# Where the feed-forward products leave their banks: behind the slot's end or behind the next slot's first step

## What is computed

```python
x = x + ln(linear_attention(ln(x)))                    # 16 heads, decay, rope
x = x + ln(ffn_int(ln(x)))                             # silu(x Wg) * (x Wu), then Wd; width 2048
x = x + ln(causal_softmax_attention(ln(x)))            # 32 heads of 16, 8 key heads, rope
x = x + ln(gated_sequence_layer(ln(x)))                # row steps, gate
```

## Time and profile before

| | us |
|---|---|
| median of 3 runs | 4023.44 (4017.86 to 4025.12) |
| the profiled execution | 4021.19 |
| its span | 4019.4 |
| granted clock of TensorE, mean | 0.959 |
| PE busy | 3665.5 (91%) |
| DVE busy | 2540.6 (63%) |
| ACT busy | 1504.4 (37%) |
| POOL busy | 1458.0 (36%) |

### The profile page before, as it was taken

One profiled execution on the slowest core, in us unless ns is written; L12 is line 12 of the kernel. 1 busy time (PEld: TensorE's weight loads), 2 busy tenths in 40 slices (PEclk: granted clock), 3 DMA queues, 4 the chain that ended last, 5 costly groups with the idle time before them and its releaser, 6 DMA issues.

```text
span 4019.4 us, 51225 instructions
## 1 busy us (share of the span) xinstructions
PE 3665.5 (91%) x18536; PEld 2701.6 (67%) x18536; DVE 2540.6 (63%) x4046; ACT 1504.4 (37%) x2349; POOL 1458.0 (36%) x1802
## 2 busy tenths in 40 slices
PE   6878899999999999999999999999999999977678
PEld 5756776677767776677767776677767776654323
DVE  6754667566764767567664766566765766466347
ACT  4423433434242434434242434434243434315124
POOL 3421452245323552245323542255323542232114
PEclk9989999999999999999999999999999999987789
DMA  6456534254324533354324433353325432332304
GB/s 244 170 196 254 199 126 146 93 201 162 137 90 157 188 117 137 105 209 142 126 101 176 175 109 136 139 189 121 136 96 197 149 137 100 116 107 74 136 18 150
DMA packets 173799, 579.00 MB, mean 144 GB/s; under 512 B 14727, under 2 KB 14983, under 8 KB 168174
## 3 DMA queue, kind: packets, MB, share of 16 engines
q1 hardware_dynamic: 169854, 568.38, 39.3%
q10 hardware_dynamic: 3696, 7.34, 0.5%
HBM read 490.21 MB, written 84.93 MB: 143 GB/s over the span
## 4 chain that ended last, share of the span: by engine, by line
PE 60%; DVE 21%; issue 7%; POOL 4%; ACT 4%; DMA 3%; SPq 0%; DVEq 0%; ACTq 0%; POOLq 0%
PE ps_P L1908 21%; PE ps_Y L1908 9%; PE ps_E L1908 6%; PE ps_T L1908 5%; PE ps_O L2142 4%; PE ps_O L1908 4%; PE ps_T L2111 3%; PE ps_E L2125 2%; DVE roped L1376 2%; DVE row_max L1574 2%; DVE ps_T L1567 2%; DVE qT_lo L1318 2%; DVE pf L1435 2%; DVE stats L1342 1%; POOL X L853 1%
## 5 line engine op out<-in xcount | busy, mean ns | idle before, releaser
L1908 PE MATMUL ps_P<-XnT_hi,w_ring 128*128 128x512 f32 x3328 | 1071.9, 403 | 41.1 <-DVE hf L1594 11.7
L1908 PEld LDWEIGHTS ps_P<-XnT_hi,w_ring 128*128 128x128 f32 x3328 | 599.8, 189 | 210.7 <-issue 76.3
L1908 PE MATMUL ps_P<-XnT_lo,w_ring 128*128 128x512 f32 x1664 | 653.7, 393 | 0.0
L860 POOL TENSOR_TENSOR pT_lo<-pf,pT_hi 128x512 fp32r<-128x512 f32 x256 | 343.8, 1355 | 390.9 <-ACT pT_hi L1034 390.9
L968 POOL TENSOR_TENSOR hT_lo<-hf,hT_hi 128x512 fp32r<-128x512 f32 x128 | 164.5, 1285 | 847.1 <-ACT hT_hi L1034 847.1
L1186 ACT ACTIVATE probs<-ps_E 128x1024 f32<-128x1024 f32 x320 | 327.5, 1023 | 295.8 <-PE ps_E L2125 295.3
L1574 DVE TENSOR_REDUCE row_max<-ps_T 128x2 fp32r<-128x768 f32 (+3 forms) x448 | 400.2, 917 | 11.0
L1567 DVE TENSOR_TENSOR ps_T<-ps_T,mask 128x512 f32<-128x512 f32 (+1 forms) x320 | 188.3, 589 | 327.8 <-PE ps_T L2111 326.3
L1908 PEld LDWEIGHTS ps_P<-XnT_lo,w_ring 128*128 128x128 f32 x1664 | 314.6, 189 | 70.2
L1908 PE MATMUL ps_Y<-w_big,hT_hi 128*128 128x512 f32 x896 | 331.5, 416 | 20.6 <-POOL hT_lo L968 7.9
L871 POOL TENSOR_TENSOR sines<-swapped,sinT 128x512 f32<-128x512 f32 x160 | 225.2, 1407 | 171.9 <-ACT swapped L1034 164.7
(11 more groups left out here) (330 smaller groups left out, 7510.6 us busy)
## 6 DMA issues: line engine op xcount, KB each, us to landing
w_ring<-split_dram SPq DMA_DIRECT2D x412, 512.0 KB, 3.4
w_big<-split_dram SPq DMA_DIRECT2D x64, 2048.0 KB, 7.7
dec<-decay SPq DMA_DIRECT2D x32, 1024.0 KB, 5.0
split_dram<-w_ring SPq DMA_DIRECT2D x58, 512.0 KB, 4.4
split_dram<-w_big SPq DMA_DIRECT2D x36, 512.0 KB, 4.4
wo1w<-split_dram SPq DMA_DIRECT2D x8, 2048.0 KB, 7.8
gatew<-split_dram SPq DMA_DIRECT2D x7, 2048.0 KB, 10.8
X<-raw_f SPq DMA_DIRECT2D x46, 256.0 KB, 4.4
```

What stands on the lines that cost most here:

```text
L860: pool.tensor_tensor(pT[1][:, k % 4, :], pf[:, k % 2, :], pT[0][:, k % 4, :].bitcast(F32), ALU.subtract).then_inc(*p_lo.hit(n, g, k))
L1908: last = pe.matmul(dst, stat[s_], mov[m_], start=first_ and k == 0, stop=last_ and k == n - 1, **kw)
```

## The change

VectorE's `product_out` for slots i = 0 to 6 is called one slot later, behind the first step of that slot; that of slot i = 7 stays at its own slot's end. ScalarE's copies of hf in slots 2, 4 and 6 move from the slot's start to its end, behind the tanh; that of slot 8 stays. TensorE, GpSimd and SyncE are not touched.

```diff
@@ ScalarE, in the loop over slots
                     q, i = divmod(s, 12)
-                    if n < NB and i in (2, 4, 6, 8):
-                        m = 4 * q + i // 2 - 1
-                        act.wait_ge(*h_f.need(n, m))
-                        copy(hT[0][:, m % IC, :], hf[:, m % 2, :]).then_inc(*h_hi.hit(n, m))
+                    if n < NB and i == 8:
+                        act.wait_ge(*h_f.need(n, 4 * q + 3))
+                        copy(hT[0][:, 3, :], hf[:, 1, :]).then_inc(*h_hi.hit(n, 4 * q + 3))
...
                         act.activation(silu[:, m % 2, :], ps["P0"][:, :], ACT.Tanh, scale=ghalf[:, m:m + 1])\
                             .then_inc(*tanh_done.hit(n, m))
+                        if i:
+                            m -= 1
+                            act.wait_ge(*h_f.need(n, m))
+                            copy(hT[0][:, m % IC, :], hf[:, m % 2, :]).then_inc(*h_hi.hit(n, m))
@@ VectorE, in the loop over slots
                     if n < NB and s % 12 >= 8:
                         product_out(n, s)
+                    if n < NB and 1 <= s % 12 < 8 and (s > 1 or c < 0):
+                        product_out(n, s - 1)
                     if c >= 0:
                         for i in steps[1:]:
                             step(c, i)
-                    if n < NB and s % 12 < 8 and (s or c < 0):
+                    if n < NB and s % 12 == 7:
                         product_out(n, s)
```

## The result

The changed kernel takes 4105.7 us in the median (4104.5 to 4112.1), the one before 4023.2 (4017.9 to 4025.1): a ratio of 1.021 (1.0193 to 1.0228), 82 us slower. The profiled execution took 4104.47 us with a span of 4102.7, 83.3 us more than before.

A forecast was written before the change was run, and what follows sets the result against it. The prediction took TensorE to bound the kernel, every new wait of it counting. Profiled 4021.2 us plus 49.7 (seven batches), 9.4 (first batch) and 22.3 (clock) gave 4103 us, range 4055 to 4130.

The forecast's parts named there:

- The masks: At the starts of slots 19 and 31, TensorE's product with V waits for GpSimd's masks: 2.5 and 2.4 us.
- The clock: TensorE's granted clock falls behind each of two mask waits: 3.4 us a batch, less 1.5 for one that goes.
- Rival 1: The mask waits come but TensorE's clock stays up: 4080 us, chance 0.22.
- rival 4: TensorE's clock also falls behind the shorter waits: 4125 us, chance 0.08.
- The banks: Query packs in slots 6, 15, 18 wait for deferred products' banks: 1.0, 0.8 us; in 18, 1.1 of 1.73 stays gained.
- maxT: VectorE's maxT copy in slots 14, 17 and 26 moves about 0.4 us later behind a product: 3 x 0.4 us.
- The other waits for row_max: In slot 27 a product no longer stands between two maxima: 0.35 us taken back of TensorE's 3.4 us.
- Slot 8: hT_lo, already waited for, comes later because hf of slot 7 follows silu of slot 6: 0.65 us.
- slot 3: At a batch's start the query pack follows layout_low, which stands behind hT_lo; the tanh ahead costs 0.5 us.
- A batch in all: Waits gained and lost in one batch sum to 7.1 us, with 3.4 us more for clock falls.
- The first batch: Products behind weight splitting, plus hT_lo: 2.8 us in second and third quarters, 3.8 in first, none in last; 9.4 us.

The follow-up runs named there:

- masks_first: Changed kernel with GpSimd's hT_lo of slots 2, 4 and 6 moved to the slot's end, behind layout and masks: 4048.7 us, ratio 1.0071.
- copy_late_only: Kernel before with only ScalarE's half of the change, copies hT_hi of slots 2, 4 and 6 behind the tanh: 4057.5 us, ratio 1.009.
- filled_wait: Changed kernel with nine extra matmuls, result overwritten, between the products with blocks 0 and 1 in slots 19 and 31: 4086.6 us, ratio 1.0159.
- first_batch_old: Changed kernel with VectorE's old order in the first batch alone, ScalarE's copies staying late: 4093.5 us, ratio 1.0179.
- banks_kept: Changed kernel with hT_lo behind the masks, VectorE's old first-batch order, and products of slots 5, 14, 17 at their own slot's end: 4009.8 us, ratio 0.9962.
- products_late_only: Kernel before with only VectorE's half of the change, ScalarE keeping its copies at the start of slots 2, 4 and 6: 4258.8 us, ratio 1.0589.

## Why the prediction came out as it did

**The masks (2.5 and 2.4 us): right.** They measure 2.29 and 2.29, by the chain given: tanh, hT_hi, hT_lo, mask, product with block 1. masks_first removes them, copy_late_only makes them alone. That GpSimd's order was "left as it is" was the heart of it: the diff has no line on GpSimd, and GpSimd's order is what costs most.

**The clock (3.4 us a batch less 1.5 in all): right in kind, a little high.** Both falls come in batch 4, to 0.52 and 0.60, and filled_wait prices them at 3.1 us. Rival 1, the clock stays up, fell. The Trainium skill's rule that stood beside it ("TensorE: Matmul & The Clock Gate", Part 1, the array falls back after a whole stretch of idleness) isn't borne out here, for the clock fell behind stretches in which TensorE was busy for 1.30 and 1.05 of 3 us; the same page's section "A second HAM failure mode: psum-queue depth-cycling", in which short idle stretches between groups of matmuls make the clock swing, is nearer to these rows. Over all seven batches 13 of the 14 mask waits are followed by a fall (the first of batch 1 is not), and copy_late_only shows that a fall behind such a wait isn't certain: 9 of 14. The shorter waits left the clock alone: masks_first keeps them, and its clock over batch 4's slots is 1.00. So rival 4 fell as well.

**The banks (0.8, 1.0 and what is left of 1.73): right in place, a little high in size.** Packs wait 0.85 us in slot 6, 0.51 in 15 and 0.56 in 18. I had 1.0 and 0.8, and for slot 18 the difference between 1.73 and 1.1.

**maxT (3 x 0.4): right.** The waits of the scores for row_max behind it are 0.37, 0.30 and 0.36. The other waits for row_max shrank from 3.4 to 2.6 us, where I had taken back 0.35. **Slot 8** is 0.8 us for 0.65, **slot 3** 0.28 for 0.5.

**A batch in all: 10.1 us in batch 4 for the 10.5 forecast (7.1 and 3.4).** The sum is closer than its parts. From first to last tanh TensorE's idle time grew from 9.3 to 14.9 us, 5.6 where the waits were to cost 7.1, and its busy time from 202.0 to 206.5, 4.5 where the clock was to cost 3.4. Of these 4.5, filled_wait puts 3.1 to the two falls; in masks_first, at a clock of 1.00, TensorE is still busy for 202.9 us, and that 0.9 has no term in the forecast. Over seven batches it is 66.9 for 72.0 (49.7 and 22.3): 0.4 in a batch like the fourth, and the fall that did not come in batch 1, which lost 8.4.

**The first batch: the term that was mis-sized.** I gave it 9.4 us and it is 16.2. I let the loads keep their times, let one product in a quarter be late by a split, and wrote "nothing in the last" quarter. The quarters lost 5.6, 5.8, 6.2 and 2.7 us. What I missed is that the splitting isn't paced by loads alone. The term had no clock in it either. Up to the second batch's first tanh, TensorE's idle time grew by 13.0 us and its busy time by 3.2. Here is the second quarter after the change:

```profile
321.80 0.70 PE L1913 MATMUL ps_P<-XnT_hi,w_ring 128*128 128x512 f32 x2 [1.25 <-DVE silu L1587]
...
324.87 0.69 ACT L1260 ACTIVATE silu<-ps_P,ghalf 128x512 f32<-128x512 f32 x1 [3.65 <-PE ps_P L1913]
...
326.63 1.37 DVE L1337 SCALAR_TENSOR_TENSOR w_ring<-probs,w_ring 128x512 fp32r<-128x512 int32 x1 [3.71 <-ACT w_ring L1056]
327.93 0.67 DVE L1587 SCALAR_TENSOR_TENSOR silu<-silu,ps_P 128x512 f32<-128x512 f32 x1
328.70 0.75 DVE L1597 SCALAR_TENSOR_TENSOR hf<-ps_P,ughalf,silu 128x512 f32<-128x512 f32 x1
...
331.51 0.50 PE L1913 MATMUL ps_Y<-w_big,hT_hi 128*128 128x512 f32 x1 [1.97 <-POOL hT_lo L968]
```

VectorE was idle for 3.71 us, but in front of the split, which waits for ScalarE's rounding of the weights, and ScalarE rounds them behind its tanh. So silu, whose tanh was over at 325.56, waits for a piece of work that itself waits for that tanh: 2.4 us from tanh to silu, where in the earlier trace rows it started as soon as the tanh released it. That is a ring through two in-order queues. It holds wherever a slot has a tanh and a split, in the last quarter too (silu starts 2.1 to 3.0 us behind the end of its tanh there), and it delays whatever stands behind it on VectorE. first_batch_old takes it away and gives 11 us back. The rest, 5 us, came with the copy behind the tanh on ScalarE, for which I had only the 0.4 us of hT_lo. TensorE's waits for hT_lo rose from 2.8 to 6.7 us, 1.6 of it by the copies alone; how much of the remaining time is theirs stays open, since it is within the spread of the traces.

So 4103 against 4105.7 is in part luck: 5 us too many in the batches and 7 too few in the first. What was foreseen is the mechanism of a batch: which waits come, where, and the falls of the clock behind the longest. Each of the large terms is within half a microsecond; that their sum is so too owes something to waits that were too high and matmul time that was too low.

## What to carry over

When a wait is put off on one in-order queue, look at the queue of whoever consumes its product: here the consumer (hT_lo) kept its place ahead of work that TensorE needs sooner, and moving the consumer along turned a loss of 36 us into a gain of 21. Put off only what stands in front of something wanted: one copy in slots with i = 6, with its hT_lo behind the masks, has shorter batches than every version with later products that was run (208.7 us; the nearest, banks_kept, has 210.4, though their whole times can't be told apart), and the kernel before with that edit (4003 us, or 4001 with all three copies) beats both versions. Don't put off the release of a bank into the slot in which another step takes that bank, nor behind work that waits for the engine that feeds it.

## What the hardware did that I had not expected

A wait of TensorE of 2.29 us, with TensorE at work before and after it, was followed in batch 4 by a granted clock of 0.52 or 0.60 over 3 us at both places, and at 13 of 14 such places in all. Its length alone doesn't decide: in copy_late_only waits of 2.30 us left the clock at 1.00 at 5 of 14 places. A wait of 1.73 us was followed by a fall once in seven batches and waits of 0.85 us not at all in the batch read. Nine throw-away matmuls in the wait kept the clock at 1.00 and made the program 19 us faster with more work in it. And in products_late_only the falls add up to a mean clock of 0.94 over a batch's slots: of the 32 us by which such a stretch is longer than in the earlier trace rows, 12.7 are matmuls that ran longer, and most of the rest is waits.
